# A conditioned mixture-of-experts kernel on one core: the shared down projection with whole float32 values, and the routing moved forward

## What is computed

```python
# layer 0: a spike count per token and channel, added to x
rates = relu(x) * 0.001
c = cond[:, None, :] + cumsum(rates, axis=1)      # along the 256 tokens of a batch
spikes = floor(c) - previous floor(c)
x = x + spikes / 0.001

# layer 1: a mixture of experts, added to x
shared = silu(xf @ w1) * (xf @ w3) @ w2           # 256 -> 512 -> 256
s = sigmoid(concat([xf, cond of the batch]) @ router_W)
topk_idx = top_k(s + router_bias, 2)              # 2 of 8 experts
gates = s[topk_idx] / (sum + 1e-9)
h = gelu(xf @ W1e); y = h @ W2e                   # 256 -> 256 -> 256 per expert
out = x + (shared + sum of gates * y) / 3
```

## Time and profile before

| | us |
|---|---|
| median of 3 runs (412.75 to 413.07) | 413.01 |
| the profiled execution | 410.6 |
| its span | 408.6 |
| shared group 3 begins | 87.19 |
| first expert transposes | 115.59 |
| first transposes of step 20 | 238.40 |
| first gather of the last stage | 314.79 |

### The profile page before, as it was taken

One profiled execution on the slowest core, in us unless ns is written; L12 is line 12 of the kernel. 1 busy time (PEld: TensorE's weight loads), 2 busy tenths in 40 slices (PEclk: granted clock), 3 DMA queues, 4 the chain that ended last, 5 costly groups with the idle time before them and its releaser, 6 DMA issues.

```text
span 408.6 us, 7282 instructions
## 1 busy us (share of the span) xinstructions
PE 320.4 (78%) x2140; PEld 294.8 (72%) x2140; DVE 238.5 (58%) x495; ACT 193.2 (47%) x320; POOL 151.1 (37%) x170
## 2 busy tenths in 40 slices
PE   0299999979689898709986069999999869796960
PEld 0178989867589897709976069999997848686850
DVE  5648879977656685606757037434332656777643
ACT  5756686685415784505754026665654312131310
POOL 2301112763874005720027500000001777777770
PEclk9998999998959999957999559999999997898975
DMA  7965345585662545233336244444422455444442
GB/s 248 298 177 156 79 95 147 184 212 142 162 193 86 149 131 166 93 114 119 106 120 227 90 129 146 132 137 153 134 73 64 123 155 154 146 150 132 147 148 78
DMA packets 38788, 58.19 MB, mean 142 GB/s; under 512 B 5216, under 2 KB 29792, under 8 KB 38752
## 3 DMA queue, kind: packets, MB, share of 16 engines
q1 hardware_dynamic: 29872, 30.98, 24.2%
q0 software_dynamic: 8880, 26.75, 23.7%
HBM read 33.59 MB, written 24.12 MB: 141 GB/s over the span
## 4 chain that ended last, share of the span: by engine, by line
PE 30%; POOL 11%; issue 6%; DMA 5%; DVE 2%; ACT 1%; SPq 1%; POOLq 0%; DVEq 0%; ACTq 0%
PE ps L1175 8%; PE ps L1176 7%; PE ps L1177 7%; POOL front L392 5%; POOL xg L392 3%; POOL x_slots L380 3%; PE ps L1322 2%; PE ps L1373 1%; DMA xg<-y_rows,y_i 1%; PE ps_d L1322 1%; DMA x_slots<-base,slot_i 1%; PE ps_d L1373 1%; DMA xg<-x_slots 1%; DVE base L1004 1%; DMA front<-y_rows,y_i 1%
## 5 line engine op out<-in xcount | busy, mean ns | idle before, releaser
L380 POOL DMA_INDIRECT x_slots<-base,slot_i x64 | 68.4, 1069 | 82.2 <-DVE slot_i L819 61.8
L1175 PE MATMUL ps<-w_hi,parts 128*128 x288 | 88.9, 309 | 1.2 <-ACT works L644 0.7
L1176 PE MATMUL ps<-w_hi,parts 128*128 x288 | 82.7, 287 | 0.0
L1177 PE MATMUL ps<-w_lo,parts 128*128 x288 | 82.5, 287 | 0.0
L1175 PE MATMUL ps<-x_hi,w_hi 128*128 128x512 f32 x128 | 55.2, 431 | 10.2 <-DMA w_lo<-w_all 5.2
L392 POOL DMA_INDIRECT xg<-y_rows,y_i x28 | 28.9, 1034 | 90.5 <-issue 90.2
L1175 PEld LDWEIGHTS ps<-w_hi,parts 128*128 128x128 f32 x288 | 57.0, 198 | 1.9 <-issue 1.9
L1176 PEld LDWEIGHTS ps<-w_hi,parts 128*128 128x128 f32 x288 | 56.9, 197 | 0.0
L1177 PEld LDWEIGHTS ps<-w_lo,parts 128*128 128x128 f32 x288 | 56.4, 196 | 0.0
L1176 PE MATMUL ps<-x_hi,w_lo 128*128 128x512 f32 x128 | 54.0, 422 | 0.0
L1177 PE MATMUL ps<-x_lo,w_hi 128*128 128x512 f32 x128 | 53.9, 421 | 0.0
(11 more groups left out here) (133 smaller groups left out, 643.4 us busy)
## 6 DMA issues: line engine op xcount, KB each, us to landing
xg<-x_slots SPq DMA_DIRECT2D x72, 128.0 KB, 2.2
y_rows<-works SPq DMA_DIRECT2D x36, 256.0 KB
w_lo<-w_all POOLq DMA_DIRECT2D x11, 512.0 KB, 7.1
x<-x_t SPq DMA_DIRECT2D x16, 256.0 KB, 3.7
xg<-w_all POOLq DMA_DIRECT2D x8, 512.0 KB, 7.6
out<-base SPq DMA_DIRECT2D x16, 256.0 KB, 2.5
base<-w_all SPq DMA_DIRECT2D x3, 512.0 KB, 6.9
x_slots<-zeros SPq DMA_DIRECT2D x1, 1024.0 KB, 17.5
```

What stands on the lines that cost most here:

```text
L380: nc.gpsimd.indirect_dma_start(x_slots, bass.IndirectOffsetOnAxis(ap=slot_i[:, k, r * RT + t:r * RT + t + 1], axis=0), base[:, rows_at(g) ...
L1175: nc.tensor.matmul(out, x_hi, w_hi, start=start, stop=False, skip_group_check=True)
L1176: nc.tensor.matmul(out, x_lo, w_hi, start=False, stop=False, skip_group_check=True)
L1177: return nc.tensor.matmul(out, x_hi, w_lo, start=False, stop=stop, skip_group_check=True)
```

## The change

The down projection's weights are no longer split: `w_down` is a plain float32 tile, loaded by SP ahead of the router's weights, and a down step is four products of the whole values `hid` by `w_down`. The ACT rounding and the DVE remainder of the hidden values, their semaphores, and one of eleven weight chunks go. `hid` has four buffers instead of two.

The routing work is placed earlier on every engine: ACT's `beside` and `experts_beside`, PE's positions of `logits`, `to_rows` and `ranks`, DVE's `FILL` and the fill in expert steps (1.6 us for steps below 13), and POOL's `expert_step` numbers. Logits of groups 4 and 5 and rows of group 4 now stand in the shared groups. Chunk numbers of the experts are one lower than before: expert e is chunk 2 + e.

The diff, cut to its core:

```diff
-    UP_S, DN_S, EXP = 0, 2 * CHUNK, 3 * CHUNK
+    UP_S, EXP = 0, 2 * CHUNK
...
+            sp.dma_start(w_down[:, :], w_all[:, NCHUNK * CHUNK:(NCHUNK + 1) * CHUNK]).then_inc(s_wdown, 16)
...
-                        expert_step(STAGE_END[r - 1] // 2 - 4 + t // 2, t % 2 == 1)
+                        expert_step(2 + t // 2 if r == 2 else 8 + t, t % 2 == 1)
...
-            def hidden_hi(g, b):
-                act_e.wait_ge(s_hid, g * SB + b + 1)
-                after(act_e, s_down, g * SB + b + 1 - SB)
-                nc.scalar.activation(hid_hi[:, b, :], hid[:, b % 2, :], ACT.Copy).then_inc(s_hhi, 1)
...
                     elif at == 7:
                         split(3)
+                        round_up(5, 0)
                         copy_rows(3, 1)
+                        split_w(7)
+                        round_up(5, 1)
+                elif g == 3:
+                    if at == 0:
                         split_w(8)
...
+                    elif at == 2:
                         split_w(9)
...
+                    elif at == 5:
+                        copy_rows(4, 0)
+                    elif at == 7:
+                        round_up(6, 0)
+                        copy_rows(4, 1)
...
-                yield from tile_list(2)
                 yield from front_scans(7)
                 yield from front_end(7, 0)
                 yield from front_end(7, 1)
+                yield from tile_list(2)
...
-                    (1.3, 1.3, 1.3, 1.3, 1.3, 0.9, 0.9, 0.9, 5.0),
-                    (1.0, 1.0, 1.2, 1.0, 1.2, 1.0, 1.2, 1.3, 4.0))
+                    (1.3, 1.6, 1.6, 1.6, 1.6, 1.3, 1.3, 1.3, 5.3),
+                    (1.0, 1.3, 1.6, 1.3, 1.6, 1.3, 1.6, 1.6, 4.3))
+            EXPERT_FILL = (1.1, 1.6)
...
                 for t in range(TT):
-                    toks = slice(t * P, (t + 1) * P)
-                    last = three(ps_d[t // 2][:, (t % 2) * C:(t % 2 + 1) * C], hid_hi[:, b, toks], hid_lo[:, b, toks],
-                                 w_hi[:, col:col + C], w_lo[:, col:col + C], b == 0 and t % 2 == 0, b == SB - 1)
+                    last = nc.tensor.matmul(ps_d[t // 2][:, (t % 2) * C:(t % 2 + 1) * C], hid[:, b, t * P:(t + 1) * P],
+                                            w_down[:, b * C:(b + 1) * C], start=b == 0 and t % 2 == 0,
+                                            stop=b == SB - 1, skip_group_check=True)
```

More of the change, by code:

```diff
@@ L536, in beside @@
                         copy_rows(1, 0)
[L537 to L549 removed]
+                        scores(0)
@@ L1121, in experts @@
                     if s > 0:
-                        beside(1.1)
+                        beside(EXPERT_FILL[s < 13])
                     if 2 <= s:
@@ L1274, in shared @@
                 if g == 0:
-                    w_ready(2)
+                    pe.wait_ge(s_wdown, 16)
                 down(g, 0)
-                if g == 2:
-                    logits(3)
-                    to_rows(3, 0)
-                up(g, 3)
-                down(g, 1)
-                if g == 2:
-                    to_rows(3, 1)
-                down(g, 2)
-                if g < 2:
-                    logits(g + 1)
-                    to_rows(g + 1, 0)
                 if g == 1:
                     ranks(0)
-                down(g, 3)
-                if g < 2:
-                    to_rows(g + 1, 1)
+                elif g == 2:
+                    to_rows(3, 0)
+                elif g == 3:
+                    to_rows(4, 0)
+                up(g, 3)
+                if g == 2:
+                    ranks(1)
+                elif g == 3:
+                    logits(5)
+                down(g, 1)
+                if g == 1:
+                    logits(2)
+                elif g == 2:
+                    to_rows(3, 1)
+                elif g == 3:
+                    to_rows(4, 1)
+                down(g, 2)
+                if g == 0:
+                    logits(1)
+                    to_rows(1, 0)
+                elif g == 1:
+                    to_rows(2, 0)
+                elif g == 2:
+                    logits(4)
+                down(g, 3)
+                if g == 0:
+                    to_rows(1, 1)
+                elif g == 1:
+                    to_rows(2, 1)
+                    logits(3)
             weights_of = {}
@@ L1415 @@
                 cols.append(w[c * P:(c + 1) * P, b * P:(b + 1) * P])
-    for b in range(w2.shape[0] // P):
-        cols.append(w2[b * P:(b + 1) * P, :])
     for e in range(E):
@@ L1421 @@
                 cols.append(w[c * P:(c + 1) * P, :])
+    for b in range(w2.shape[0] // P):
+        cols.append(w2[b * P:(b + 1) * P, :])
     arrays = {
```

149 lines of the change are left out of this document (56 added, 93 removed), and 2 rows, old and new, of the table FILL.

## The result

The changed kernel takes 391.08 us (median of 3 runs, 390.78 to 392.07), against 413.01 before: ratio 0.948, 95% interval 0.945 to 0.950. The forecast was 392, range 381 to 402. Ratios in this text are taken over the fast runs of both kernels, and can differ by up to 0.005 from the quotient of the two medians shown beside them. On a second chip that acted alike it was 391.89 us against 412.07 (0.952, interval 0.941 to 0.963).

A forecast was written before the change was run, and what follows sets the result against it. POOL's gathers bound the last stage; before it PE was mostly busy, with two stalls for unscattered rows in the expert steps. Span 408.6 + 9.0 - 29.8 = 387.8 us, median 392, range 381 to 402.

The forecast's parts named there:

- Part 1: Down steps of the shared groups: whole-value products cost PE 0.46 us more each, +7.4 us for sixteen before the experts.
- Part 2: Groups 0 to 2: dearer down steps, logits, rank products and new waits, +8.0 us; group 3 starts at 95.1.
- Part 3: Group 3: ACT's row copy waits for late scatters, PE stands 6 us; group lasts 29.5 us, experts start +9.0.
- rival A: Group 3: ACT's copy does not hold the last silu, expert 7's load or the scan being earlier; 385 us, chance 0.18.
- Part 4: Steps 0 to 20: earlier scatters remove stalls of 11.7 and 17.3 us and one low-clock restart of 2.8.
- So I charge nothing: Steps up to 14: DVE's fuller load adds no time, 63.4 us against 63.3 in the trace without stall and restart.
- Rival C: Steps 1 to 12: DVE is the bound at 4.4 us a step, 8 us more, 400 us; chance 0.16.
- rival D: Shared groups: whole-value down products do not keep the clock up; slower than before, up to 478 us; chance 0.05.
- Part 5: Before step 20: SP's late pad clears leave a stall of 7.3 us, with a low-clock restart already in the trace.
- The rest: Step 20 to the end: stays at 170.2 us, its last 94 us going by POOL.
- B: Step 20: pads cleared in time or quicker SP reads; 7.3 us and the 2.8 restart go, 382 us; chance 0.09.
- E: Expert steps: the two stalls only move to another wait of the same size, 410 to 413 us; chance 0.02.

The follow-up runs named there:

- pads_spread: Changed kernel with four of eight pads cleared with the request for step 15 and four with that for 17: 382.1 us against 408.5 of before, 0.933.

## Why the prediction came out right, and where it did not

**Part 1, the down product.** Right in kind, a third too dear in size. The four products are recorded as eight instructions, and the next product starts 1.72 us behind the first (PE's timeline, group 1 of the changed kernel):

```profile
56.40 1.89 PE L1184 MATMUL ps_d<-w_down,works 128*128 128x256 f32 x8
58.12 0.33 PE L1223 MATMUL ps_r<-member,earlier 128*128 128x64 f32 x2
```

That is 0.215 us for a record, between the bounds (0.115 and 0.23) and near the one I took; the price is 1.72 - 1.37 = 0.35 us a step, not 0.46, so 5.6 us instead of 7.4 for sixteen steps. A whole-value product (two records) thus takes 0.43 us, a rounded one of the same columns 0.12, 3.6 times less; the Trainium skill ("FP8 and Floating Point Precision", TensorE Precision Notes) gives true FP32 four passes, and the trace agrees with that nearly. What the edit takes away I booked as 1.3 us of waits in groups 0 to 2 and, together with the routing, 7.4 us in group 3, 8.7 in all. The edit alone shortens the four groups by 4.1 us, price included, so it takes away 9.7 us.

**Part 2, groups 0 to 2.** Forecast 95.1 for the start of group 3, measured 94.28. The two new waits were 0.8 us for the prefix and 0.8 us for a row copy, forecast 0.9 and 0.6. The price was 4.2 us instead of 5.5; against that group 0 itself began 0.8 us later (19.95 instead of 19.13), behind a longer wait for its weights (5.8 us against 5.2), which was in no term.

**Part 3, group 3.** The chain is right, each of its lengths was too long. The split of expert 7 ended 12.4 us into the group (forecast 13.7), the copy of the rows of group 4 ran 19.9 us into it (22.6), PE waited 3.6 us for it (6), and the down steps behind it ran at the low clock, 4.5 us for two. Group 3 lasted 26.0 us, not 29.5. The term that failed most is "8.9 us from the split to the last scatter"; it was 7.4 (106.7 to 114.15). Part of rival A came true by that, for its own reason.

**Part 4, steps 0 to 20.** The stall before step 12 went, as forecast, and with it its restart. But step 14 came 71.4 us behind the start of the experts, not 63.4. "So I charge nothing" is the step that failed; and steps 1 to 12 lasted 5.4 us each, which the prediction had named as a sign of being wrong. Windows of steps 0 to 14 of the kernel before, of its stall before step 12, and of its steps 0 and 1; then steps 0 to 14 of the changed kernel in its first and its second trace:

```profile
115.59:193.36 77.77, 61.94 (x470) 60.48 (x471) 41.99 (x107) 38.44 (x69) 26.36 (x27) 0.86 0.41 130
171.26:183.01 11.75, 0.01 (x1) 0.00 (x1) 0.90 (x2) 1.39 (x3) 4.48 (x5) 0.67 0.31 100
115.59:120.63 5.04, 5.04 (x24) 5.04 (x25) 2.52 (x5) 1.19 (x2) 3.82 (x5) 0.50 0.74 240
120.63:126.27 5.64, 5.64 (x38) 5.64 (x38) 2.52 (x10) 2.97 (x4) 4.12 (x5) 0.69 0.26 94
```

```profile
120.25:191.60 71.35, 60.71 (x462) 58.61 (x460) 54.02 (x140) 39.80 (x70) 38.36 (x36) 0.90 0.48 155
120.85:192.52 71.67, 59.73 (x462) 57.30 (x461) 53.92 (x140) 39.90 (x70) 38.59 (x37) 0.93 0.48 156
```

The 8 us are mostly time in which PE had nothing to do: 10.6 us (71.35 less 60.71) against 4.1 before beside the stall (77.77 less 61.94 less 11.75). The waits there are 3.4 us for row copies, 2.6 for prefixes and 1.5 for the sums of group 3, of which I had counted none, and 2.9 us ahead of tile transposes that the profile puts down to nothing (before 1.3, nothing, nothing and 1.0).

The low clock is a smaller part than it looks. Windows of steps 2, 6 and 8 of the changed kernel:

```profile
129.41:133.70 4.29, 4.29 (x20) 4.29 (x21) 1.98 (x3) 1.20 (x2) 1.72 (x2) 0.50 0.26 92
151.69:157.42 5.73, 5.73 (x37) 5.73 (x37) 2.75 (x11) 2.03 (x4) 4.21 (x6) 0.70 0.54 178
166.08:171.15 5.07, 5.07 (x33) 5.07 (x34) 2.62 (x10) 1.69 (x3) 0.89 (x1) 0.71 0.12 38
```

A clock of 0.50 through step 2, 0.70 in step 6 and 0.71 in step 8 cost 2.1 + 1.7 + 1.5 = 5.3 us against full clock. But the kernel before lost 2.5 + 1.7 = 4.2 us in the same way in its steps 0 and 1, and these are in the 63.3 us that I took as the measure. The second trace shows how the two belong together: its clock is higher (0.93), PE had nothing to do for longer (11.9 us), and the time is the same. So it is in seven of the eight undisturbed traces with the routing moved: from step 0 to step 14 they take 71.4 to 72.8 us, with a clock of 0.88 and 9.4 us without work at one end and 0.93 and 13.0 at the other. The eighth (`pads_spread`) takes 68.8.

So something other than PE's own speed sets these steps. Rival C had the size (+8 us), and in part the mechanism: DVE is busy 54.0 of the 71.35 us (42.0 of 77.8 before), 3.9 us a step and not the 4.4 that C reckons with, so its load alone doesn't fill the steps of 5.1 us. But PE waits for its prefixes and sums, and where the rank products were moved out of the way of the prefixes, PE waited for DVE's remainders, ACT's row copies and tiles instead, and gained nothing. That the order of the work on DVE and ACT is the limit is the reading that fits; an experiment that moves that order itself was not made.

What brought the clock down is shown in part. Before steps 2 and 8 PE stood: 1.5 us for the sums of group 3 and 2.1 for a prefix, then 2.1 for a row copy. Before step 6 it stood 1.3 us for a row copy and 0.3 more, and ran a row of whole-value logits (sixteen records of 8 columns). The changed kernel, then `pads_spread` at the same place:

```profile
149.30 0.28 PE L1160 MATMUL ps<-w_lo,parts 128*128 x1
149.82 1.92 PE L1202 MATMUL ps_r<-rw,x 128*128 128x8 f32 x16 [0.25 <-issue]
...
152.54 0.41 PE L1159 MATMUL ps<-w_hi,parts 128*128 x1
```

```profile
151.76 1.92 PE L1203 MATMUL ps_r<-rw,x 128*128 128x8 f32 x16 [0.25 <-issue]
153.62 0.63 PE L1318 MATMUL ps<-ident,xg 128*128 128x128 f32 x4
```

In the first the products behind the logits take 0.41 us instead of 0.28. In the second the same waits and the same row stand ahead, the clock stays at 1.00 and step 6 takes 4.2 us instead of 5.7. Of the eight traces four have the one and four the other, and two rows of logits behind a PE without waits in the kernel before (155.20 and 197.09) left the clock at 1.00. So rival D's mechanism is not shown in this place either: the low clock can follow such waits and such a row, and need not. Behind the down products it doesn't come (the clock is 1.00 in groups 1 and 2, whose down products are all whole values).

**Part 5, the stall before step 20.** Forecast 7.3 us, measured 8.1, with the clears where they were said to be; and 10.2 us came back when they were split. From the changed kernel, answering:

```profile
207.41 0.38 SPq L306 DMA_DIRECT2D y_rows<-works  x1
209.40 5.42 SPq L281 DMA_DIRECT2D x_slots<-zeros  x8
219.46 0.92 SPq L300 DMA_DIRECT2D xg<-x_slots  x2
...
SPq L293 <- DMA x_slots<-zeros: 3.1, 1, 3.1
```

The clears landed 3.1 us behind the last issue instead of 1.6, and were themselves 0.2 us shorter; from store to tile load it was 12.05 us where I had 11.1, which makes the difference.

**The rest.** 167.9 us instead of 170.2. The cover held, as forecast: sixteen dearer down steps cost nothing there. That the gathers themselves would be quicker was in no term.

The total is right by luck: two misses of 4.3 and 2.3 us the one way stand against 9.1 the other. The median came nearer still (391.1 for 392) by a second piece of it: I added 4.4 us from span to median, of which 2.4 said only that the execution profiled before was a quick one, and this time the median lies 0.8 above the span. Of the rivals, A came partly, by another mechanism than told; C came in size and partly in mechanism; B's condition did not hold; D fell; E fell.

## What to carry to other kernels

An edit that frees the engine that another edit loads should be costed together with it, stage by stage (1.1% and 2.5% alone, about 5% together; the traces have 3.7 us of that ahead of the experts). When work moves on an in-order queue, read what stands behind it: eight clears moved three steps forward moved their stall with them, four and four had none. When work is packed more densely, the trace of before is no measure of what its engines will wait for: here PE stood 6.6 us more in fourteen steps, which no sum of loads had shown. And before a low clock is charged with lost time, look for the same loss in the kernel before, and for a second trace in which the clock held.

## What the runs showed of the hardware that I had not expected

- A whole-value product of 128x256 is two records, 0.215 us from start to start, against 0.12 us for one of rounded parts.
- Four clears of 128 KB in a row leave SP's queue in 1.92 us (0.48 each); eight in a row take 5.4 to 6.3 us (0.68 to 0.79 each). Why the later ones take longer the traces don't show.
- The same sixteen narrow whole-value products behind the same waits of PE were followed by a clock of 0.70 in four traces and of 1.00 in four others.
- The 64 gathers of 128 rows held POOL 62.2 to 63.4 us where DVE had 45.6 to 45.9 us of work in the stage, 65.1 and 65.2 where it had 56.1 and 56.2.
- One of the three chips ran the kernel before 4 to 5% slower than the others (428.3 against 408.5 to 413.0), with waits of the same length in different kernels (25.2 us ahead of one silu in three of four). What it waited for, its traces don't show.
